# Second attention: the reciprocals and the mixing after the softmax move from one pair behind the search to two, in the same buffers

## What is computed

```python
dots = jnp.einsum('bhid,bhjd->bhij', q, k) * scale          # k, v: 16 memory rows, then 512 tokens
dots = jnp.einsum('bhij,hk->bkij', dots, pre_proj)          # first mixing
dots = jnp.where(causal[None, None], neg, dots)
top = lax.top_k(dots, SPARSE_TOPK)[0]                       # 64
dots = jnp.where(dots < top[..., -1:], neg, dots)
attn = jax.nn.softmax(dots, axis=-1)
attn = jnp.einsum('bhij,hk->bkij', attn, post_proj)         # second mixing
out = jnp.einsum('bhij,bhjd->bhid', attn, v)
```

## Time and profile before

| | us |
|---|---|
| median of 3 timed runs | 4224.01 (4220.88 to 4232.35) |
| profiled execution, its own time | 4254.16 |
| its span in the trace | 4252.3 |
| VectorE busy | 2504.3 (59%) |
| TensorE busy | 3085.7 (73%) |
| GpSimd busy | 967.3 (23%) |
| ScalarE busy | 1066.9 (25%) |
| granted TensorE clock, mean | 0.783 |

### The profile page before, as it was taken

How to read it: one execution, slowest core, us unless ns; L and a number is a source line. 1 busy time by engine, 2 the same in 40 slices (tenths; PEclk the granted TensorE clock), 3 DMA queues, 4 the chain that set the end, 5 groups by cost and what they waited for, 6 DMA issues and landing times. The chain is left out here.

```text
span 4252.3 us, 41618 instructions
## 1 busy us (share of the span) xinstructions
PE 3085.7 (73%) x12160; PEld 1887.1 (44%) x12160; DVE 2504.3 (59%) x7782; ACT 1066.9 (25%) x2741; POOL 967.3 (23%) x1212
## 2 busy tenths in 40 slices
PE   4747973997576777777677765443797855999997
PEld 2324552775343454455345444321233532555554
DVE  5994654551359989997999899568433141111112
ACT  1114531341133333333334332211001110111111
POOL 2540003002034544444444444200220000000000
PEclk6558986998657868767777866765898956999999
DMA  2000004554122122111212111000100003000000
GB/s 78 0 0 15 4 18 167 165 162 133 55 81 73 45 74 65 63 59 59 74 44 77 49 58 30 25 5 0 53 0 20 3 2 99 0 0 0 0 0 20
DMA packets 158964, 199.66 MB, mean 47 GB/s; under 512 B 30750, under 2 KB 133731, under 8 KB 158758
## 3 DMA queue, kind: packets, MB, share of 16 engines
q1 hardware_dynamic: 155686, 188.85, 14.1%
q0 software_dynamic: 3072, 8.39, 0.6%
HBM read 136.12 MB, written 61.08 MB: 46 GB/s over the span
## 5 line engine op out<-in xcount | busy, mean ns | idle before, releaser
L2058 DVE MATCH_REPLACE8 a_rest<-a_best,a_rest 128x416 f32<-128x416 f32 (+54 forms) x1308 | 605.0, 471 | 0.0
L2066 DVE MAX8 a_best<-a_rest 128x8 f32<-128x416 f32 (+54 forms) x1308 | 566.3, 475 | 0.0
L1736 PE MATMUL a_pmix<-a_rows,a_kpre 128*128 128x264 f32 (+41 forms) x528 | 244.7, 606 | 380.0 <-ACT a_mixed L1860 375.3
L2000 POOL TENSOR_SCALAR a_probs<-a_mixed,a_best 128x120 f32<-128x120 f32 (+12 forms) x208 | 285.7, 1373 | 377.5 <-DVE a_best L2070 354.2
L2843 DVE TENSOR_TENSOR e_hT<-e_act_out,e_pc 128x512 f32<-128x512 f32 x128 | 88.0, 687 | 478.4 <-ACT e_act_out L2834 472.8
L1736 PEld LDWEIGHTS a_pmix<-a_rows,a_kpre 128*128 128x128 f32 x528 | 123.7, 274 | 431.0 <-issue 423.6
L1745 PE MATMUL a_pat<-a_kp,a_probs 128*128 128x128 f32 x1344 | 261.2, 361 | 53.4 <-POOL a_kp L1962 48.5
L1745 PEld LDWEIGHTS a_pat<-a_kp,a_probs 128*128 128x128 f32 x1344 | 235.0, 262 | 126.7 <-POOL a_kp L1962 73.1
L2797 PE MATMUL e_ph<-xT,e_w 128*128 x512 | 244.4, 600 | 55.8 <-PEq L2760 46.7
L1726 PE MATMUL a_psc<-a_kT,branch 64*128 64x264 f32 (+3 forms) x640 | 234.8, 641 | 27.4 <-ACT a_stage L1827 26.6
L2814 PE MATMUL e_py<-e_w,e_hT 128*128 128x256 f32 x1024 | 254.4, 391 | 0.0
(11 more groups left out here) (448 smaller groups left out, 5608.0 us busy)
## 6 DMA issues: line engine op xcount, KB each, us to landing
f_w<-in_L_ffn_W SPq DMA_DIRECT2D x39, 1024.0 KB, 5.8
l_scores<-a_stage SPq DMA_DIRECT2D x32, 528.0 KB, 2.7
l_scores<-a_stage SPq DMA_DIRECT2D x32, 400.0 KB, 2.4
l_scores<-a_stage SPq DMA_DIRECT2D x32, 272.0 KB, 2.1
f0o_w<-in_L_ffn_W SPq DMA_DIRECT2D x8, 1024.0 KB, 12.5
sorted_x<-z_blank SPq DMA_DIRECT2D x1, 4992.0 KB, 17.1
f_xs<-sorted_x SPq DMA_DIRECT2D x39, 128.0 KB, 5.4
sorted_y<-f_ys SPq DMA_DIRECT2D x39, 128.0 KB, 5.7
```

The source lines that it names most:

```text
L1736: ins = pe.matmul(pmix[:, at, 0:hi - lo], kpre[:], rows[:, g % 4, lo:hi], start=True, stop=True)
L2000: ins = pool.tensor_scalar(p, x, best[:, a, LAST, 7:8], HIDE, ALU.is_lt, ALU.mult)
L2058: last[a] = signal(dve.match_replace(rest[:, a, 0:wd], best[:, a, q - 1, :], rows_of[a] if q == 1 else rest[:, a, 0:wd], GONE))
L2066: last[a] = signal(dve.max(best[:, a, q, :], rest[:, a, 0:wd]))
```

## The change

Reciprocal, scaled matrix, second mixing and its copy move from pair `k - 1` to pair `k - 2` in step `k`; the exponentials stay at `k - 1`. The loops of TensorE and ScalarE get one more step. GpSimd scales the matrix before the memset of a block's first two pairs, and both behind the two cuts. The products with the values (`l1_heads`) of blocks at the second to fourth place of a batch row start one step later, with two of them in the block's last step. No buffer is added.

```diff
@@ l1_heads
     if n == GROUPS1 - 1:
-        return [(n, j) for j in range(8)] if s == 0 else []
+        return [(n, j) for j in range(8)] if s == 1 else []
     if n % NT == 0:
         return [(n, 2 * (s - 2) + a) for a in range(2)] if 2 <= s < 6 else []
-    return [(n, s)]
+    return [] if s == 0 else [(n, s - 1)] if s < STEPS1 - 1 else [(n, s - 1), (n, s)]
@@ TensorE
-                for k in range(-2, PAIRS1 + 1):
+                for k in range(-2, PAIRS1 + 2):
...
                     for a in range(2):
-                        if k >= 1:
-                            post(2 * (k - 1) + a)
+                        if k >= 2:
+                            post(2 * (k - 2) + a)
@@ ScalarE
-                for k in range(-1, PAIRS1 + 1):
+                for k in range(-1, PAIRS1 + 2):
                     for a in range(2):
-                        if k >= 1:
+                        if 1 <= k <= PAIRS1:
                             exps(2 * (k - 1) + a)
...
-                        if k >= 1:
-                            post_out(2 * (k - 1) + a)
+                        if k >= 2:
+                            post_out(2 * (k - 2) + a)
@@ GpSimd
+                    if k >= 2:
+                        weights(k - 2)
+                    for a in range(2):
                         g = 2 * k + a
                         if k >= 0 and s < 2:
                             if g >= 4:
                                 pool.wait_ge(post_full, g - 3)
                             i = l1_group(n)[1]
                             pool.memset(probs[:, g % 4, i * P:(i + 2) * P], 0.0).then_inc(zeroed, 1)
-                    if k >= 1:
-                        weights(k - 1)
...
+                weights(PAIRS1 - 2)
                 weights(PAIRS1 - 1)
@@ VectorE
-                        if q == min(rounds[0], TOP1 // 16) and pair >= 1:
-                            invert(pair - 1)
+                        if q == min(rounds[0], TOP1 // 16) and pair >= 2:
+                            invert(pair - 2)
+                invert(PAIRS1 - 2)
                 invert(PAIRS1 - 1)
```

More of the change, by code:

```diff
@@ L2046, in _ @@
                     if lanes[0][2] <= TOP1:
-                        if pair >= 1:
-                            invert(pair - 1)
+                        if pair >= 2:
+                            invert(pair - 2)
                         continue
```

## The result

The changed kernel takes 4327.01 us (median of 4, 4315.74 to 4340.16) against 4228.18 of the kernel before on the same chip (4220.88 to 4232.86): 99 us slower, ratio 1.024, 95% interval 1.0209 to 1.027. The forecast was 4287 in a range of 4250 to 4325. Direction and place were right, the size was not: 63 us forecast, 99 measured.

A forecast was written before the change was run, and what follows sets the result against it. VectorE's search was taken to set the pace. Batch-row changes 41.4, block 1 beginnings 17.7, start 0.6 and end 2.9 sum to +62.6, say 63 us, on the timed median 4224: 4287, range 4250 to 4325.

The forecast's parts named there:

- What bounds: Second attention: VectorE's search sets the pace, time changes only where VectorE stands still; the search's own durations stay unchanged.
- The removed wait: VectorE's 131.0 us wait at the reciprocal (L2029) for the previous pair's exponentials: removing it is worth 0, at most -21.
- the first kind: Waits at a batch row's first pairs: worth 0, VectorE would wait for the next scores anyway, at L2045 instead.
- the second: Waits in mid-search where block 1 begins: 21 us at most, kept only if read-out 49 is not later; taken as 0.
- The loop: Room for two pairs of weights closes a loop from read-out through second mixing, comparison and exponentials; steps 60-63 add 3.6, 0.1, 1.7, 1.0.
- The changes of batch row: Three places, around pair 65 and its likes, where read-outs come late without slack: 15.2, 13.1 and 13.1, together +41.4 us.
- The beginnings of block 1: Four places, around pairs 49 to 51 and their likes: late read-outs cost 5.5, 5.1, 5.1 and 2.0, together +17.7 us.
- The clock: TensorE possibly held at lower clock: +6.6 for step 61 and likes, as much again for projections; about 13 above the sum, 4300.
- The tail: End of the stage: pair 126's second mixing, twelve instructions, comes behind the last search too, +2.9 us.
- No change: Rival: slack before pair 65 swallows the delay; only tail and starts remain, +3 to +10, so 4231; chance 0.05.
- faster: Rival: mid-search waits really saved, 21 us less plus 3.5 at the ends, about 4207; chance 0.04.
- Binds more widely: Rival: loop exceeds the pair in blocks 3 and 2 too; with lower clock some 4 us more at 11 places, +107, 4331; chance 0.11.

The follow-up runs named there:

- the kernel with six tiles: The changed kernel with room for six tiles of weights (three pairs) instead of four, scores' rows and small tiles cut to make room: 4244.88 us, ratio 0.9963.
- the idle products: The changed kernel plus two 128x512 products that nothing reads at the end of each step of blocks 3, 1 and 2: 4272.52 us, ratio 1.0026.
- the one with the second mixing first: The changed kernel with TensorE's second mixing ahead of the step's side work, ScalarE copying in the same order: 4269.38 us, ratio 1.0022.
- the one with the order alone: The kernel before, lag of one pair, with products with the values a step later and GpSimd's scaled matrices ahead of the memsets: 4229.89 us, ratio 1.0004.

## Why the prediction was right and wrong

**What bounds.** Right. VectorE's search sets the pace; its own busy time in the search moved by 8 us, 1395.5 to 1403.6 (most of it in `max` and `match_replace` of the same shapes, 1171.3 to 1177.3, for which I have no explanation; I had forecast no change), and the rest of the 99.7 is waiting.

**The removed wait.** Right for the first kind: the row at L2029 went and the time came back at L2047. For the second, 21 us at most, I wrote "kept only if read-out 49 is not later than before". It was later, nothing was kept, and the kernel with six tiles shows that it could have been: 12 of the 21.

**The loop.** Right, and shown from three sides: opened by buffers, shortened by the order, kept pace with by a faster TensorE. The steps 60 to 63 were given 3.6, 0.1, 1.7 and 1.0 us; they measured 2.7, 3.9, 1.7 and 1.1. Three are near; step 61 is off by 3.8 us, and that one is the clock (its score products alone took 2.57 us longer).

**The changes of batch row, +41.4; measured +56.2.** Most of the 14.8 missing are step 61 and its likes, at 1.2 GHz throughout: 3.8 us in the second and third row. I had priced that case ("+6.6") and left it out of the sum. For the first row I had read that step 29 "runs at the lower clock throughout", and that was wrong: its first mixing was slow (2.98 us), but its score products took 4.92 us and its second mixing 1.60. After the change they took 7.37 and 2.93, so this row lost in the same way, and I had added only 2.1 there. The rest had gathered before: by pair 56 and its likes the comparison was 1.2 to 3.2 us late, where I began at 0.

**The beginnings of block 1, +17.7; measured +45.0.** The worst term, and the parts show why. Pairs 17, 49, 81 and 113 start 4.4, 2.1, 4.4 and 2.1 us later, where I had 0: the loop entered block 1 some 5 to 7 us behind instead of 2.2. Pair 51 and its likes cost 6.2, 6.1, 6.1 and 2.9, near the 5.1 and 2.0. "From pair 52 on the loop keeps up with pairs of over 9 us" was false: read-outs 51 to 53 came 10.7 and 11.0 us apart, against pairs of 9.2 and 9.7, so pairs 52 and 53 lost 2.9 more in each of three rows. The eight projections of steps 50 and 51 took 5.29 and 4.78 us where they had taken 3.60. With the idle products they took 3.60 again, and pairs 52 and 53 lost 0.1 us (0.9 in the first row).

```profile
1790.60 0.98 PE L1736 MATMUL a_pmix<-a_rows,a_kpre 128*128 128x216 f32 x4 [0.53 <-ACT a_mixed L1860]
1791.41 3.60 PE L1698 MATMUL a_psc<-xT,a_w 128*128 128x512 f32 x8
...
1798.81 3.60 PE L1698 MATMUL a_psc<-xT,a_w 128*128 128x512 f32 x8
```

(before, steps 50 and 51) and after the change:

```profile
1806.42 0.99 PE L1736 MATMUL a_pmix<-a_rows,a_kpre 128*128 128x216 f32 x4 [2.34 <-ACT a_mixed L1860]
1807.24 5.29 PE L1698 MATMUL a_psc<-xT,a_w 128*128 128x512 f32 x8
...
1818.55 4.78 PE L1698 MATMUL a_psc<-xT,a_w 128*128 128x512 f32 x8
```

**The clock: the step that failed.** "My sum takes each step at the clock that it had", "+6.6" beside it for step 61 and its like, and "as much again" for the projections. After the change TensorE waits in the very steps that had been fast, 2.3 us ahead of step 50's first mixing instead of 0.5, 3.7 ahead of step 61's instead of 1.0. Its clock is lower in them and its side work longer, and that work is now part of the loop, so that every slow step delays the next read-out. I priced this as a surcharge on single steps and left it out of the sum.

What takes the clock down is not the same in both places. In steps 50 and 51 it goes with the closed loop: their projections took 5.29 and 4.78 us in the changed kernel, and 3.60 each in the kernel with six tiles, in the one with the second mixing first, and in the one with the order alone. That is what a feedback would look like, waiting that slows TensorE and so makes more waiting. In step 61 the score products took 7.37 us in those three kernels as well. There the new order is enough, and the loop only makes it count.

The runs put about 90 of the 99 us on a clock below what the idle products restore. That is more than the miss of 36, because part of my 63 was itself worked out from steps that were slow already before, such as 58 to 60 (granted clock of step 58: 0.50). The Trainium skill ("TensorE: Matmul & The Clock Gate", "HAM oscillation") describes such a fall and return for a wait on DMAs. The trace agrees in kind: TensorE waits for ScalarE's read-out here, not for a DMA, and the clock in step 61 goes from 1.00 to 0.50 with a wait of 3.73 us ahead of it where 0.99 was. I followed the page for the direction, and then bounded it by a few steps a row.

**The tail.** +2.9 forecast, +1.4 measured: the twelve instructions of pair 126 cost their 2.93 us, but TensorE, by then at a granted clock of 1.00, did the sixteen of pair 127 behind them in 1.95 instead of 3.50:

```profile
2783.20 2.93 PE L1745 MATMUL a_pat<-a_kp,a_probs 128*128 128x128 f32 x12 [6.13 <-POOL a_kp L1962]
...
2791.11 1.95 PE L1745 MATMUL a_pat<-a_kp,a_probs 128*128 128x128 f32 x16
```

**The rivals.** "No change" and "faster" were wrong for the reasons given. "Binds more widely", at 4331, came nearest in number (4327) and had the clock in it. It was right in asking for more at each place (3.5 to 9.0 us, where it had 4), wrong in adding four places at block 3, which cost nothing (-0.8 to +0.1).

## What to carry to other kernels

Before a step is moved a turn later, ask which buffer its input occupies and who refills it: a lag of two in room for two makes every stage of the turn one loop, and its length is then to be compared with the turn of the engine that sets the pace, turn by turn. If TensorE is in that loop, work the loop out at the lower clock, in all its steps; what a closed loop costs is not read from the clock that the open one had. Moving work within the steps can by itself swap fast steps of TensorE for slow ones (4.80 us to 7.37 here), and as long as the loop is open that does not show in the time. Where neither buffers nor order can give the slack back, a few idle products in TensorE's pauses can; in the kernel before, with its open loop, they bought nothing that could be told.

## What the runs showed of the hardware

Two idle products a step, 2.0 us of TensorE at a clock of 1.00, raised the granted clock from read-out 56 to read-out 64 from 0.67 to 0.89 and made the stretch 12 us shorter (107.0 us against 119.0). Without them:

```profile
1854.60:1973.60 119.00, 88.00 (x356) 58.97 (x356) 114.02 (x384) 42.26 (x134) 49.38 (x68) 0.67 0.19 63
```

and with them:

```profile
1842.20:1949.20 107.00, 86.82 (x388) 53.88 (x388) 107.00 (x365) 42.19 (x133) 49.53 (x68) 0.89 0.21 71
```

There are 16 more products (32 instructions), and TensorE's busy time is lower than without them. The same sixteen score products took 4.80 us at a granted clock of 1.00 and 7.37 at 0.50. In the kernel with the idle products there are steps where the clock changed on the way: 5.99 us at a mean of 0.78, and 6.64 at 0.61.
